# Two attention layers on a sorted graph: bins and slots loaded into registers for sixteen steps at once

## What is computed

```python
def conv(x, src, dst, qw, qb, kw, kb, vw, vb, sw, sb):   # H = 2 heads, D = 128
    q, k, v = ((x @ w + b).reshape(N, H, D) for w, b in ((qw, qb), (kw, kb), (vw, vb)))
    alpha = jnp.einsum('ehd,ehd->eh', q[dst], k[src]) / sqrt(D)
    m = jax.ops.segment_max(alpha, dst, num_segments=N)
    ex = jnp.exp(alpha - m[dst])
    w = ex / (jax.ops.segment_sum(ex, dst, num_segments=N)[dst] + 1e-16)
    agg = jax.ops.segment_sum(w[:, :, None] * v[src], dst, num_segments=N)
    return agg.mean(axis=1) + x @ sw + sb
h = conv(x, src, dst, *layer1) + x @ lin1_w + lin1_b
out = conv(h, src, dst, *layer2) + h @ lin2_w + lin2_b
return layernorm(x + out)
```

## Time and profile before

| | |
|---|---|
| time, median of 3 runs | 1224.38 us (1219.8 to 1226.35) |
| time of the profiled execution | 1224.0 us |
| its span | 1222.2 us |
| busy: PE, DVE | 998.6 us (82%), 981.6 us (80%) |
| busy: ACT, POOL | 786.5 us (64%), 756.7 us (62%) |
| TENSOR_LOADs on PE, on DVE | 208, 208 |

### The profile page before, as it was taken

How to read it: one execution, slowest core, us unless ns; L and a number is a source line. 1 busy time by engine, 2 the same in 40 slices (tenths; PEclk the granted TensorE clock), 3 DMA queues, 4 the chain that set the end, 5 groups by cost and what they waited for, 6 DMA issues and landing times.

```text
span 1222.2 us, 32117 instructions
## 1 busy us (share of the span) xinstructions
PE 998.6 (82%) x6792; PEld 774.2 (63%) x6792; DVE 981.6 (80%) x5260; ACT 786.5 (64%) x2594; POOL 756.7 (62%) x804
## 2 busy tenths in 40 slices
PE   4778989888787879788986787879787888788887
PEld 3546767666575667677754565657665666666775
DVE  5798889988787888899486777777787878878876
ACT  1356658777585868676274464748576758677655
POOL 7777777777777777300077777777777777771000
PEclk9988989999898999999896898998999989999988
DMA  5333333333333333100132332323233323330001
GB/s 141 87 77 90 87 79 88 80 90 79 79 79 79 81 80 79 45 1 2 44 108 77 83 80 70 88 72 89 74 85 76 84 79 80 79 81 23 2 2 53
DMA packets 51941, 87.04 MB, mean 71 GB/s; under 512 B 16699, under 2 KB 25169, under 8 KB 51761
## 3 DMA queue, kind: packets, MB, share of 16 engines
q0 software_dynamic: 25024, 51.30, 17.3%
q1 hardware_dynamic: 24145, 32.62, 9.6%
q10 hardware_dynamic: 2592, 1.07, 0.3%
HBM read 81.58 MB, written 3.34 MB: 69 GB/s over the span
## 4 chain that ended last, share of the span: by engine, by line
PE 27%; issue 18%; DVE 18%; POOL 17%; DMA 15%; ACT 3%; DVEq 2%; SPq 0%; POOLq 0%; ACTq 0%
POOL gathered L424 17%; PE ps L703 13%; DMA gathered<-h_rows,src_e 7%; DMA gathered<-in_x,src_e 7%; PE ps L691 7%; DVE junk L972 6%; DVE acc L1003 5%; PE ps L794 2%; ACT whot L525 2%; PE ps L789 1%; PE ps L778 1%; DVE apart L983 1%; DVE max_b L1041 1%; DVEq L1003 1%; DVEq L972 1%
## 5 line engine op out<-in xcount | busy, mean ns | idle before, releaser
L703 PE MATMUL ps<-gathered,whot 128*128 x3328 | 568.1, 298 | 82.4 <-ACT whot L525 50.4
L525 ACT ACTIVATE whot<-apart,below 128x128 f32<-128x128 bf16 x1664 | 551.4, 388 | 129.5 <-DVE apart L983 114.4
L703 PEld LDWEIGHTS ps<-gathered,whot 128*128 128x128 f32 x3328 | 453.8, 198 | 162.0 <-issue 124.6
L972 DVE SCALAR_TENSOR_TENSOR junk<-ps,gathered 128x129 f32<-128x129 f32 x1664 | 413.6, 286 | 152.2 <-issue 80.9
L691 PE MATMUL ps<-table,hot_t 128*128 x2496 | 440.3, 287 | 76.5 <-DVE junk L972 49.9
L424 POOL DMA_INDIRECT gathered<-in_x,src_e x391 | 377.7, 966 | 119.8 <-issue 84.8
L424 POOL DMA_INDIRECT gathered<-h_rows,src_e x391 | 374.2, 957 | 119.0 <-issue 82.3
L1003 DVE TENSOR_TENSOR acc<-ps,acc 128x258 f32 x832 | 350.5, 421 | 21.6 <-PE ps L703 12.6
L691 PEld LDWEIGHTS ps<-table,hot_t 128*128 128x128 bf16 x2496 | 250.9, 101 | 168.6 <-issue 125.0
L509 ACT ACTIVATE apart<-col_b,ndl_e 128x128 bf16<-128x128 bf16 x618 | 239.1, 387 | 0.0
L972 DVE DVE_READ_ACCUMULATOR junk<-ps,gathered 128x1 f32 x1664 | 135.7, 82 | 0.5
(11 more groups left out here) (176 smaller groups left out, 551.4 us busy)
## 6 DMA issues: line engine op xcount, KB each, us to landing
dl_bc<-local_dst_rows SPq DMA_DIRECT2D x104, 256.0 KB
gathered<-in_x,src_e POOLq DMA_INDIRECT x391
gathered<-h_rows,src_e POOLq DMA_INDIRECT x391
h_rows<-table SPq DMA_DIRECT2D x6, 256.0 KB, 2.3
out<-x_rows SPq DMA_DIRECT2D x6, 256.0 KB
table<-in_L_gnn_q_w ACTq DMA_DIRECT2D x2, 128.0 KB
table<-in_L_gnn_k_w ACTq DMA_DIRECT2D x2, 128.0 KB
wv<-in_L_gnn_v_w ACTq DMA_DIRECT2D x2, 128.0 KB
```

The costliest lines, as they stand in the source:

```text
L525: last = nc.scalar.activation(whot[:, c % UN, h, :], apart[:, c % UN, :], ACT.Exp, scale=FAR, bias=below[:, j % 2, h, o:o + 1])
L703: last = nc.tensor.matmul(bank_u[n % NB][:, h * C1:(h + 1) * C1], whot[:, c % UN, h, :], gathered[:, bass.ds(slot, 1), :].rearrange("p o c ...
L972: last = V.scalar_tensor_tensor(out=junk[:, t % 2, h, :], in0=bank_t[n % NB][:, h * C1:(h + 1) * C1], scalar=1.0, in1=gathered[:, bass.ds( ...
```

## The change

One constant is changed. Four places are governed by it: the lengths of the two loads and, on PE and DVE, the steps at which they are made. Loads at multiples of 8 that are no multiples of 16 go away, and each of the others fills 16 registers instead of 8. `BC` (the step count of a one-hot block) has a constant of its own and stays 8.

```diff
 RING = 98
 UN = 4
-RB = 8
+RB = 16
 BC = 8
 GQ = 8
```

## The result

The change makes the kernel slower: 1230.46 us in the median of 17 runs (1226.13 to 1233.79), against 1224.51 us for the kernel before (17 runs, 1219.8 to 1228.07). The ratio is 1.0046, with a 95% interval of 1.0035 to 1.0058. The forecast was 1219.3 us, so it was wrong in the sign. The prediction took 0.5% for what can't be told from none; with so many runs, 0.46% is clear of it.

A forecast was written before the change was run, and what follows sets the result against it. The prediction took POOL's gathers to pace each layer, with engine time counting only in the tails. From 1224.0 us profiled, -5.6 (removed loads) + 0.7 (dearer loads) - 0.2 (ring) gave 1218.9, or 1219.3 for the median; range 1215.5 to 1227.

The forecast's parts named there:

- What bounds the kernel: POOL's unbroken gathers, about 1.26 us apart, pace each layer; engine time counts only in some 80 us after alpha step 384.
- rival 4: Engines, not POOL, pace the layers, so half of DVE's 80.9 us idle ahead of L972 goes: 1184 us; chance 0.02.
- What the change removes: DVE's idle time behind removed loads near both layers' ends goes: 2.99 and 2.58 us, together 5.57 us.
- What the change adds: The 7 loads staying on DVE in each layer's tail cost 0.05 us more each: 0.7 us; break-even 0.40 us extra.
- rival 2: Registers are paid one by one, 0.59 us extra a load; tails +2.7, early first layer +2.8: 1229.9 us; chance 0.10.
- the tails: Some 80 us ending each layer, from alpha step 384, where engines run late by themselves and saved time moves the end.
- PE's loads: In the tail, PE's loads are as many as DVE's at neighbouring places; nothing was added for them.
- The ring: Gathers waiting for old u steps early in the first layer cost 0.17 us; shorter engine queues give that back, -0.2 us.
- Rival 3: Gathers meet DVE's instructions differently, redrawing 11.3 us of excess: 1216.5 or 1222.1 us; chance 0.15 of over 2 us.
- Rival 1: In the tail, half the removed idle time returns as waits for PE or ACT; gain 2.1 us: 1222.3 us; chance 0.15.

The follow-up runs named there:

- e9: Kernel before plus 32 register loads of 1 to 24 registers behind DVE's last instruction; single execution: 4 took 0.35 us, 8 0.60, 16 1.10.
- e17: Loads of sixteen registers with the gathers' ring widened from 98 to 104 slots, against the kernel before: 1227.73 us, ratio 1.0026.
- e4: Only PE loads sixteen registers, DVE stays at eight, against the kernel before: 1231.23 us, ratio 1.0055.
- e3: Only DVE loads sixteen registers, PE stays at eight, against the kernel before: 1229.21 us, ratio 1.0035.
- e1: Both engines load four registers at once instead of eight, against the kernel before: 1222.45 us against 1225.57, ratio 0.9981.
- e5: The change again, sixteen registers on both engines, against the kernel before at 1225.24 us: 1229.73 us, ratio 1.0048.

## Why the prediction was wrong, step by step

- **What bounds the kernel** was read rightly. The gathers run at their own pace in every trace at 1224 to 1232 us, and only the ends of the layers and the full ring let the engines' time through. Half as many loads didn't bring back half of the 80.9 us (rival 4): the same row stands at 89.0 us in the change.
- **What the change removes** was right. The gaps behind loads 392 and 408 are gone.
- **What the change adds: the extra for 16 registers** is the step that failed, "I take a value near the lower end, 0.05 us". It measured 0.50 us on DVE and 0.51 on PE. The argument for it was the narrow spread of the durations, "a round trip of fixed length, not eight of them". The 591 ns are a fixed part and two equal ones, one for each four registers: e9 shows 0.25 us for each. A narrow spread tells nothing of how many equal parts a time has. All rows of before had the same size, so they had no say in it; rival 2, with bounds from the same row, deserved at least the forecast's chance. Put into the prediction's own sum, 14 x 0.50 - 5.57 gives +1.4 us for the tails. The other half of the term held: the seven loads in each layer pay the extra about in full (+7.45 us over the two layers, and 14 x 0.50 is 7.0).
- **PE's loads** were "the same number and lie at neighbouring places; I add nothing". This is the second failing step, and it fits the tails' loss of 3.2 us (e17; 3.8 in the first trace, where DVE's gaps behind its own loads account for 1.9). A load of 0.59 us on PE was covered at step 400; one of 1.10 us isn't (0.34 us left), and e4 loses 0.55% by PE's loads alone. The engines hand work to each other through three banks and four weight buffers, so a longer stall of either can stop both. That e3 and e4 each cost as much as the two together is seen; that their stalls coincide is inferred from it and from the two engines' loads standing at neighbouring steps.
- **The ring** was in the sum as -0.2 us and in rival 2 as "+2.8 us, all of it passed to POOL because the ring has no slack". The rival was right that the ring passes something on: 0.20%, 2.4 us, with the doubt of 2 us named above (change and e17).
- **Rival 2** as a whole gave 1229.9 us; 1230.46 was measured. Its decision point of 0.40 us was passed. Its chance of 0.10 was the mistake. That it hit the time so closely is partly luck: it had the extra at 0.59 us where 0.50 was measured, and PE's loads at nothing, like the forecast. **Rival 3**, the redraw of the gathers, is real in single traces: the second layer's gathers take 490.3 to 492.6 us over all traces at the usual pace. It is at most some 2 us. It may be part of why the profiled execution of the change lies 3 us under the median, but most of the 3.2 us that the gathers' durations lost there isn't a redraw of meetings: the median gather took 944 ns instead of 947, which is 2.3 us over 782 of them. That DVE's instructions make some gathers longer wasn't tested. **Rival 1**, idle time that returns as waits for PE, can't be told apart from the effect of PE's dearer loads.
- **The Trainium skill's** rate in "Runtime: NRT & Kernel Launch", "Instruction fetch mechanics", of about 200 ns a register was set aside since 8 took 591 ns. That section of the Trainium skill gives it beside the preamble, where the runtime loads registers; the loads here are the kernel's own, from on-chip memory. e9 agrees with it for single registers (0.20 to 0.26 us each) and not for aligned fours (0.25 us together). The Trainium skill's floor of about 600 ns in "DMA: Bandwidth & Descriptors", "Latency and other measured facts", isn't one: 4 registers take 0.35 us.

What stays open: why loads of four win only 0.19% (e1), though its trace has no wait for the ring and less idle time of DVE in the tails (6.3 and 7.3 us against 7.8 and 8.0); its loads take more queue time in all (143 against 124 us on DVE). And how large the ring's waits are on average without the wider ring, as each trace gives another number. And what part the granted clock has: its mean is 0.931 over the 17 runs of the change and 0.939 over the 24 runs of before beside e5. It can't be the whole cause, since the runs of e1 have 0.931 too and are faster than before, but no run holds the clock fixed. No version beat the kernel before by more than e1 does.

## What to carry to other kernels

A register load is paid in its engine's queue and by its length in one piece: the engine hides only what it still holds of work already handed over, here 0.1 to 0.6 us of DVE's loads of 1.10 us, and where the engine is behind the rest is lost, it seems for its neighbours too. So fewer and longer loads are no saving where the price goes by register; make them as short as their groups allow, and aligned. Here that was worth 0.2% (e1). And where every row of a trace has one size, run one other size before costing a change of size.

## What the runs showed of the hardware

A load of registers from on-chip memory took 0.10 us + 0.25 us for each aligned group of four, and 0.20 to 0.26 us for each register outside one (e9, on DVE); two registers (0.54 us) cost more than four (0.35 us), and eight that start at element 2 cost three times as much as eight that start at element 0 (1.85 against 0.60 us).
